# Expert stage: finished rows added straight into the output by an indirect transfer, instead of gathered back at the end

## The reference, cut to what matters

```
top_v, top_i = top_k(softmax(x @ gate_w.T), 2)      # 2 of 8 experts per token
comb_w[token, e] = top_v where e was chosen, else 0
for e in range(8):
    h = silu(x @ w1[e] + b1[e])                     # 512 -> 2048
    y = h @ w2[e] + b2[e]                           # 2048 -> 512
    out = out + y * comb_w[..., e]
t = t + out
```

## Time and profile before

| | |
|---|---|
| median of three runs | 1652.41 us (1646.14 to 1654.00) |
| the profiled execution | 1653.27 us |
| its span, first to last instruction | 1651.7 us |
| expert stage, first block's layer 1 begins | 1151.80 us |
| last matmul of the kernel ends | 1616.01 us (1605.64 + 10.37) |
| PE / DVE / ACT / POOL busy, share of the span | 80% / 67% / 43% / 22% |

### The profile page before, as it was taken

How to read it: one execution, slowest core, us unless ns; L and a number is a source line. 1 busy time by engine, 2 the same in 40 slices (tenths; PEclk the granted TensorE clock), 3 DMA queues, 4 the chain that set the end, 5 groups by cost and what they waited for, 6 DMA issues and landing times.

```text
span 1651.7 us, 34685 instructions
## 1 busy us (share of the span) xinstructions
PE 1327.7 (80%) x12878; PEld 911.1 (55%) x12879; DVE 1107.4 (67%) x1725; ACT 712.4 (43%) x1091; POOL 356.5 (22%) x366
## 2 busy tenths in 40 slices
PE   3734799999358999974659999865999999998991
PEld 1214576765256676642235555452677777776770
DVE  3576888887668888866876666654646775476333
ACT  3236455454545545531263323241646664466330
POOL 0121344544223454340220000005000000000004
PEclk9857899999678999986959999955999999999996
DMA  8042000000310000014021000025436663354005
GB/s 291 30 148 95 2 2 1 1 1 1 130 37 3 1 1 1 1 51 154 25 67 47 1 0 0 0 105 220 170 126 229 224 227 125 129 199 152 25 26 159
DMA packets 34029, 132.31 MB, mean 80 GB/s; under 512 B 6664, under 2 KB 8456, under 8 KB 24016
## 3 DMA queue, kind: packets, MB, share of 16 engines
q1 hardware_dynamic: 25808, 103.19, 17.3%
q0 software_dynamic: 8160, 28.32, 5.0%
HBM read 108.82 MB, written 22.68 MB: 80 GB/s over the span
## 4 chain that ended last, share of the span: by engine, by line
PE 47%; issue 17%; DVE 16%; POOL 11%; DMA 4%; ACT 4%; POOLq 0%; DVEq 0%; SPq 0%; ACTq 0%
PE banks L2138 14%; PE banks L2159 13%; PE banks L1670 5%; PE banks L1700 3%; POOL mb_quad L942 2%; POOL mb_ysq L906 2%; DVE mb_ca L592 2%; POOL mb_quad L934 1%; POOL mb_ring L929 1%; POOL mb_ysq L892 1%; PE banks L1002 1%; POOL xs_table L2171 1%; DVE mb_S L679 1%; PE banks L340 1%; DMA eb_un<-ys_table,eb_slot 1%
## 5 line engine op out<-in xcount | busy, mean ns | idle before, releaser
L2138 PE MATMUL banks<-eb_x_hi,eb_w_hi 128*128 128x128 f16 x1344 | 228.3, 220 | 2.0 <-DVE eb_x_lo L2038 2.0
L2138 PE MATMUL banks<-eb_x_lo,eb_w_hi 128*128 128x128 f16 x1344 | 228.3, 220 | 0.0
L2138 PE MATMUL banks<-eb_x_hi,eb_w_lo 128*128 128x128 f16 x1344 | 228.2, 220 | 0.0
L978 PE MATMUL banks<-mb_u_hi,mb_wi_hi 128*128 (+3 forms) x1152 | 204.2, 223 | 4.8 <-ACT mb_ca L805 4.8
L978 PE MATMUL banks<-mb_u_hi,mb_wi_lo 128*128 (+3 forms) x1152 | 203.8, 222 | 0.0
L978 PE MATMUL banks<-mb_u_lo,mb_wi_hi 128*128 (+3 forms) x1152 | 203.8, 222 | 0.0
L2138 PEld LDWEIGHTS banks<-eb_x_hi,eb_w_hi 128*128 128x128 f16 x1344 | 132.3, 98 | 4.7 <-issue 2.4
L2138 PEld LDWEIGHTS banks<-eb_x_lo,eb_w_hi 128*128 128x128 f16 x1344 | 132.3, 98 | 2.4
L2138 PEld LDWEIGHTS banks<-eb_x_hi,eb_w_lo 128*128 128x128 f16 x1344 | 132.3, 98 | 0.0
L2159 PE MATMUL banks<-eb_w_hi,eb_h_hi 128*128 x336 | 128.4, 382 | 0.0
L2159 PE MATMUL banks<-eb_w_lo,eb_h_hi 128*128 x336 | 128.2, 382 | 0.0
(11 more groups left out here) (437 smaller groups left out, 3238.7 us busy)
## 6 DMA issues: line engine op xcount, KB each, us to landing
eb_raw<-e_w SPq DMA_DIRECT2D x36, 1024.0 KB, 5.0
eb_un<-e_w SPq DMA_DIRECT2D x28, 1024.0 KB, 7.4
mb_ring<-m_in_w SPq DMA_DIRECT2D x8, 1072.0 KB, 5.3
xs_table<-zero POOLq DMA_DIRECT2D x1, 6400.0 KB, 21.1
eb_xg<-xs_table POOLq DMA_DIRECT2D x23, 256.0 KB, 2.9
ys_table<-eb_y POOLq DMA_DIRECT2D x21, 256.0 KB, 6.7
ab_raw<-a_in_w SPq DMA_DIRECT2D x4, 1154.0 KB, 11.7
mb_ring<-m_out_w SPq DMA_DIRECT2D x4, 1024.0 KB, 5.2
```

The lines of the kernel that those rows point to most:

```text
L978: x = e.matmul(ps[0:width, bank, n * P:(n + 1) * P], a[:, k, f:f + width], b[:, k, ds(i * P, P)], start=(k == 0 and m == 0), stop=(k == KD ...
L2138: o = e.matmul(ps[:, j, c * P:(c + 1) * P], a[:, side, k, f * P:(f + 1) * P], b[:, k, :], start=(k == 0 and m == 0), stop=(k == KD - 1 and ...
```

## The change

POOL no longer writes blocks to `ys_table`. It writes each block's 128 rows by an indirect transfer with `compute_op=ALU.add` into the output tensor itself, at the tokens' rows. For that the row's token number and gate must be known in the block's order. They go there by a small table in DRAM, `who_table`, with two numbers (8 bytes) for each slot: DVE puts the gates beside the token numbers in `mine`, POOL scatters them by 16 indirect transfers of 128 x 8 bytes, waits for them, and loads the table back as `who` (128 partitions x 23 blocks x 2). DVE copies a block's token numbers to `row` as integers and multiplies the block by the gates as it leaves PSUM. SP stores the residual tiles to `out` before the blocks instead of at the end; POOL waits for these stores before its first block. Slots that no token fills point, with gate 0, at 128 spare rows behind the output, which the host drops. The first stage fills `who_table` and the spare rows in place of a part of `ys_table`. A fifth small load, `c_mine`, joins the stage's parameter loads, for all of which `par_in` stands.

```diff
@@ zero_tables
-        e.dma_start(self.ys_dram[TOPK * TT * P:(FILLED - 2) * P, :].rearrange("(b p) f -> p b f", p=P),
-                    zero[:].unsqueeze(1).to_broadcast([P, FILLED - 2 - TOPK * TT, D])).then_inc(self.zero_out, 16)
+        e.dma_start(self.who_dram[0:FILLED * P, :], self.ins["c_nobody"]).then_inc(self.zero_out, 16)
+        e.dma_start(self.out[TOK:TOK + P, :], zero[:]).then_inc(self.zero_out, 16)
@@ stage_moe
-    PARS = ((gw, "e_gw"), (b1, "e_b1"), (b2, "e_b2"), (iota, "c_iota"))
+    PARS = ((gw, "e_gw"), (b1, "e_b1"), (b2, "e_b2"), (iota, "c_iota"), (mine, "c_mine"))
@@ sp: between the loads for the second expert and the loop of loads
+        e.wait_ge(b2_done, TT)
+        for i in range(TT):
+            e.dma_start(core.out[i * P:(i + 1) * P, :], t[:, i, :]).then_inc(t_sent, 16)
...
-        for i in range(TT):
-            e.wait_ge(t_done, TOPK * (i + 1))
-            e.dma_start(core.out[i * P:(i + 1) * P, :], t[:, i, :]).then_inc(out_sent, 16)
-        e.wait_ge(out_sent, 16 * TT)
+        e.wait_ge(t_sent, 16 * TT)
@@ dve: behind the plan
+        for k in range(TOPK):
+            x = e.tensor_copy(mine[:, k * TT:(k + 1) * TT, 1], top[:, :, k])
+        x.then_inc(mine_done, 1)
@@ dve: end of a block
+            e.wait_ge(who_in, 16)
             core.apart(e)
-            e.tensor_copy(y[:], ps[:, 5, :]).then_inc(y_ev, 1)
+            e.tensor_copy(row[:], who[:, ds(s, 1), 0])
+            e.tensor_scalar(y[:], ps[:, 5, :], who[:, ds(s, 1), 1], None, ALU.mult).then_inc(y_ev, 1)
@@ dve: behind the blocks
-        for n in range(TOPK * TT):
-            i, k = n // TOPK, n % TOPK
-            e.wait_ge(back[n % TT], 16 * (n // TT + 1))
-            if k:
-                e.wait_ge(t_done, n)
-            e.scalar_tensor_tensor(out=t[:, i, :], in0=un[:, n % TT, :], scalar=top[:, i, k:k + 1], in1=t[:, i, :],
-                                   op0=ALU.mult, op1=ALU.add).then_inc(t_done, 1)
@@ pool: behind fetch(1)
+        e.wait_ge(mine_done, 1)
+        for k in range(TOPK):
+            for i in range(TT):
+                e.indirect_dma_start(out=who_dram, out_offset=bass.IndirectOffsetOnAxis(ap=slot[:, k, i:i + 1], axis=0),
+                                     in_=mine[:, k * TT + i, :], in_offset=None).then_inc(told, 16)
+        e.wait_ge(told, 16 * TT * TOPK)
+        e.dma_start(who[:, 0:MOST, :], who_dram[0:MOST * P, :].rearrange("(b p) c -> p b c", p=P)).then_inc(who_in, 16)
+        e.wait_ge(t_sent, 16 * TT)
@@ pool: block
-            e.dma_start(ys_dram[ds(s * P, P), :], y[:]).then_inc(y_out, 16)
+            e.indirect_dma_start(out=core.out, out_offset=bass.IndirectOffsetOnAxis(ap=row[:, 0:1], axis=0),
+                                 in_=y[:], in_offset=None, compute_op=ALU.add).then_inc(y_out, 16)
@@ pool: behind the blocks
-        for n in range(TOPK * TT):
-            i, k = n // TOPK, n % TOPK
-            if n >= TT:
-                e.wait_ge(t_done, n - TT + 1)
-            e.indirect_dma_start(out=un[:, n % TT, :], out_offset=None, in_=ys_dram[0:(FILLED - 2) * P, :],
-                                 in_offset=bass.IndirectOffsetOnAxis(ap=slot[:, k, i:i + 1], axis=0)).then_inc(back[n % TT], 16)
```

More of the change, by code:

```diff
@@ L59, in __init__ @@
         self.xs_dram = nc.dram_tensor("xs_table", [TABLE * P, D], F32).ap()
-        self.ys_dram = nc.dram_tensor("ys_table", [TABLE * P, D], F32).ap()
+        self.who_dram = nc.dram_tensor("who_table", [TABLE * P, 2], F32).ap()
         self.zero_set, self.zero_out = self.sem("zero_set"), self.sem("zero_out")
@@ L273, in pool @@
         e.wait_ge(added, TT)
-        e.wait_ge(core.zero_out, 32)
+        e.wait_ge(core.zero_out, 48)
     def act(e):
@@ L1818, in stage_moe @@
     y = sb("y", [P, D])
-    xs_dram, ys_dram = core.xs_dram, core.ys_dram
+    mine, who, row = sb("mine", [P, TOPK * TT, 2]), sb("who", [P, TABLE, 2]), sb("row", [P, 1], U32)
+    xs_dram, who_dram = core.xs_dram, core.who_dram
     names = """par_in var_done sd_done un_done turned0 copied0 logits max_done exp_done mask_done ranks table_done plan_done
-         scattered xg_in turned xhi_done xlo_done whi_done wlo_done h_mm h_taken silu_done hhi_done
-        hlo_done y_mm y_ev y_out t_done y_sent out_sent mix_done mix_turned mix_ev b2_mm b2_done dve_own act_own""".split()
+         mine_done told who_in t_sent scattered xg_in turned xhi_done xlo_done whi_done wlo_done h_mm h_taken silu_done hhi_done
+        hlo_done y_mm y_ev y_out y_sent mix_done mix_turned mix_ev b2_mm b2_done dve_own act_own""".split()
     s_ = {n: sem(n) for n in names}
     (par_in, var_done, sd_done, un_done, turned0, copied0, logits, max_done, exp_done, mask_done, ranks, table_done, plan_done,
-     scattered, xg_in, turned, xhi_done, xlo_done, whi_done, wlo_done, h_mm, h_taken, silu_done,
-     hhi_done, hlo_done, y_mm, y_ev, y_out, t_done, y_sent, out_sent, mix_done, mix_turned, mix_ev, b2_mm, b2_done, dve_own, act_own) = \
+     mine_done, told, who_in, t_sent, scattered, xg_in, turned, xhi_done, xlo_done, whi_done, wlo_done, h_mm, h_taken, silu_done,
+     hhi_done, hlo_done, y_mm, y_ev, y_out, y_sent, mix_done, mix_turned, mix_ev, b2_mm, b2_done, dve_own, act_own) = \
         (s_[n] for n in names)
     raw_in = [core.sem(f"e_raw_in{b}") for b in range(EX_RAWS)]
-    back = [sem(f"back{b}") for b in range(TT)]
-    PARS = ((gw, "e_gw"), (b1, "e_b1"), (b2, "e_b2"), (iota, "c_iota"))
+    PARS = ((gw, "e_gw"), (b1, "e_b1"), (b2, "e_b2"), (iota, "c_iota"), (mine, "c_mine"))
     PAR = 16 * len(PARS)
@@ L2301, in shape_constants @@
     c["c_iota"] = np.tile(np.concatenate([np.arange(E), 1 - 2 * (np.arange(E) % 2), np.arange(MOST)]).astype(np.float32), (P, 1))
+    token = np.arange(TT)[None, :] * P + k[:, None]
+    c["c_mine"] = np.tile(np.stack([token, 0 * token], 2), (1, TOPK, 1)).astype(np.float32)
+    c["c_nobody"] = np.tile(np.stack([TOK + k, 0 * k], 1), (FILLED, 1)).astype(np.float32)
     return c
@@ L2347 @@
     ins = {k: nc.dram_tensor(k, v.shape, mybir.dt.from_np(v.dtype), kind="ExternalInput").ap() for k, v in arrays.items()}
-    out = nc.dram_tensor("out", [TOK, D], F32, kind="ExternalOutput").ap()
+    out = nc.dram_tensor("out", [TOK + P, D], F32, kind="ExternalOutput").ap()
     program(nc, ins, out)
     result = run_bass_kernel_spmd(nc, [arrays], core_ids=[0]).results[0]["out"]
-    return np.ascontiguousarray(np.asarray(result).T).reshape(1, SEQ, SIDE, SIDE)
+    return np.ascontiguousarray(np.asarray(result)[:TOK].T).reshape(1, SEQ, SIDE, SIDE)
```

## The result

The changed kernel takes 1639.08 us (median of 12 runs, 1634.01 to 1644.00), beside 1653.91 for the kernel before (12 runs, 1646.14 to 1657.98): a ratio of 0.9914, with an interval of 0.9893 to 0.9934. It is faster by 0.9%, where 1630, or 1.4%, was forecast.

What follows compares the result with a forecast made beforehand. PE sets the pace through the blocks, then 35.7 us of copying, writing, gathering and adding follow. From 1653.27: -27.5 end, +3.0 `who`, +0.3 parameter load, +0.7 gaps, -23.5 in all, giving 1629.8, called 1630; range 1623 to 1645.

Steps and rivals of the forecast that it cites:

- the tail's sum: After the last matmul: steps from 1616.01 add up to 1624.2 instead of 1651.7, gaining 27.5 us, bounds 23.2 to 28.8.
- about 0.3 for the last waits: Kernel's end, behind POOL's loop: the last waits take about 0.3 us, beside 1.94 for leaving the loop.
- stores of the residual ... `t_sent` costs nothing: Before the blocks: SP's 2 MB of stores land long before POOL finishes its scatters, so waiting for them costs nothing.
- longer loop bodies may lengthen the gaps: PE's gaps without a releaser, such as 2.65 and 4.21 us, may grow: 0.7 us added, from 0 to 2.
- Gaps without a releaser that weren't there: In the profile after: listed among the signs that would show the forecast wrong; no size given.
- the table is there in time: Rival, start of the blocks: the table lands by 1184.5, its load needing 8.5 us; total 1626.8, chance 0.25.
- the 3.0 us for `who`: First blocks: `who` lands at 1186.5, PE waits 2.0 us, plus 1 for the clock; bounds 0 to 15.3.
- DVE's train: Start of the blocks: DVE's subtractions from 1170.76 hold the 16th scatter until 1173.9, but not the table load's issue.
- The adding transfer isn't the bound: Each block: the add hides under PE's 21.1 us; the rival, 22 us landings and about 1692, had chance 0.07.
- The table's rival of 1642: Rival, first blocks: the table is slow, PE waits 12.5 us and its clock falls; chance 0.12 with 1636 to 1645.
- the rival of about 1652: Rival: the end hardly shortens, or something else takes the gain; 1645 to 1661, chance 0.06.
- the prediction's own case of 1627 to 1636: Whole kernel: a small wait of PE for the table, forecast 1630 us, chance 0.50.

Runs made afterwards that it cites:

- x1: The changed kernel without the eight stores of the residual, so the output lacks the residual: median 1638.6 us, ratio 0.9916 to the kernel before.
- x5: The changed kernel with each residual store issued as soon as its tile is ready, ahead of the second expert's weight loads: 1630.25 us, ratio 0.9869 to before.
- x8: The changed kernel with early residual stores and a POOL drain in every block together: median 1623.6 us, ratio 0.9832 to the kernel before.
- x4: The changed kernel with the residual stores issued later, once PE has turned block 1: 1630.01 us, ratio 0.9878 to the kernel before.
- x2: The changed kernel without the 16 short scatters of token and gate, all rows then going to spare rows: 1629.47 us, one execution.
- x11: The changed kernel, unchanged, profiled once more: 1640.16 us, one execution.
- x7: The changed kernel with the blocks' rows scattered without the add, so the sum is left out: 1629.97 us, one execution.
- x6: The changed kernel with a POOL drain in every block, between the fetch and the wait for y: median 1628.03 us, ratio 0.9872 to before.
- x9: The changed kernel with early stores, drains in every block and no table, token and gates riding in `xs_table` rows: median 1625.35 us, ratio 0.9820 to before.
- x10: The kernel before, unchanged, profiled once more: 1646.38 us, one execution.

## Why the prediction was right or wrong

The end, the mechanism. The 16 gathers went as worked out, and the first half of the tail's sum holds: from the last matmul to the empty bank 1.25 (predicted 1.19), leaving the loop 1.9 (1.94). POOL's issue came 1.07 after the copy (0.76). The adding transfer took 4.7, beside the 4.0 chosen between 2.7 and 8.3. The Trainium skill, Collectives: The Full Stack, on SDMA and CCE, led to an estimate of 4.05. The landings of the last transfer, 4.7 with the add and 2.8 without, are a ratio of 1.7 where it would be 1.5; 0.6 of the 1.9 between them is issue, so that less than this speaks of the datapath.

**The step that failed at the end** is "about 0.3 for the last waits": behind the loop stands POOL's drain, and it cost 5.7, with 0.3 beside it. In the kernel before that drain was already there and ended beside the last store, so the chain didn't show it; its row is longer, 14.1 us from 1637.3, but POOL was still issuing gathers until 1643.6, so that less than this is clearing up. With it the gain at the end is 20.7, not 27.5, and it falls outside the bounds of 23.2 to 28.8, which moved only the transfer. The difference of 6.8 is 5.7 of drain, 0.7 of transfer, 0.3 of handing over and 0.1 of rounding.

**The step that failed at the start** is "stores of the residual ... `t_sent` costs nothing", and with it the 16 scatters, which were counted by POOL's time alone. Nobody waited for the stores' semaphore, that part was right. But the question was asked only of who waits for them, not of what else travels by the DMA engines. The term "longer loop bodies may lengthen the gaps", 0.7 with a bound of 2, named the right gap with the wrong cause: it is 4.3 to 4.8 longer, and what follows it is slower too, up to 7.0 in all. That second part the prediction knew and put elsewhere: it has layer 2 slower by 2.16 behind a gap of 4.21, at a granted clock of 0.53, but it charged this only to the wait for `who` and took the gap of 2.65 for one that costs nothing behind it. "Gaps without a releaser that weren't there" was given as a sign that the forecast is wrong, and it is what appeared.

**The table.** POOL's scatters went as predicted, 0.96 + 0.30 each, but for the 1 us that DVE's short subtractions were to add: the longest is 1.04. The load was issued at 1176.81 (predicted 1176.0). The rival "the table is there in time" is the one that came true: the load took 5.0, with 1.5 of issue, not 10.5, so the 3.0 us for `who` were none. The 32 ns for each 8-byte run were too much: the trace has the 2944 runs in 48 packets of 448 or 512 bytes, of 0.14 to 0.56 us each. The rest is luck: SP issued the next weights only at 1180.01, 3.2 behind the start of the load, since PE's longer gap had held DVE up. Where they come 0.4 to 0.9 behind it, the load takes 7.4, 7.8 and 8.1 (x1, x5, x8), and 9.7 in x4 (0.4 ahead of it, behind the late stores), near the 10.5. The last scatter wasn't held up by DVE's train, since that came later (1177.53) than before: a term that was right only while everything else stood still. The 4.23 us that POOL waited for the scatters to land (1.7 predicted) and a stage that began 1.5 later stand in its place, so that the start agrees by errors that cancel. The load's issue wasn't held by DVE's train: 1.54 us, with the train from 1177.53 on beside most of it, for 1.50 in x2, where it ran without one.

**The rest.** The parameter load, 0.3, is 0: what PE does there isn't later. The adding transfer isn't the bound, with 21.1 us of cover for at most 8.3; row copy and scale hide under PE. The table's rival of 1642 and the rival of about 1652 did not occur in their way, though the second one's form ("something else takes the gain") describes what happened at half its size.

Two of the prediction's bounds are a little off in themselves: 28.8 moves only the transfer, and without most of the row copy it would be 29.0; and with 20 us for each microsecond the 27.5 of the end last to a landing of 20.3, the 20.1 being for the net gain.

The sum after the event, against -23.5: end -20.7, start of the blocks +7.0 (of which 2.2 are the clock), stage begun later +1.5, parameter load and table 0: -12.2. The missing half is two terms, 6.8 and 7.0, of which neither is a wait on a semaphore. The 4.0 us that the prediction added for the table, the parameter load and the gaps didn't occur, and hid that much of the two. That 1639.08 lies within 1623 to 1645 is in part luck: it is outside the prediction's own case of 1627 to 1636, in the stretch that was held by a slow table, and the table wasn't slow.

Still open: by what the stores hold the instruction transfers up and the short scatters stretch them; why the clock stayed up behind the gap in one profile of 13; what lowers it in the attention-like block in some executions and not in others; and what in POOL's earlier transfers the drain works off (with plain scatters it took 6.35).

## What to carry to other kernels

When work moves from the end into a quiet stretch, ask what comes through that stretch besides what waits for a semaphore: an engine that jumps over a long piece of its program for the first time may stop until code has come by DMA. Without the 16 short scatters and the 2 MB of stores the gap was 2.5, with the one 3.8 to 4.4, with the other 4.7 to 5.9, with both up to 7.5, though nobody waits for either, and the clock then takes up to 2.6 more (x8). When two kernels are compared by profile, look at the granted clock of the stretch before, too: it moved the start of this stage by up to 10 us. When the last transfers of an engine become the end of the program, look for the instructions behind the loop that the chain of waits never showed, such as a drain, and do their work inside the loop, where it is covered. Two numbers for each row cost PE less when they were carried in the row itself than in a table of their own (a gap of 2.49 for 3.80), though the times of the two kernels can't be told apart.

## What the runs showed of the hardware

- POOL's drain depends on what POOL's transfers have left behind: 5.70 us at the end of this kernel and of x1, x4, x5 and x11 (6.35 in x7), 5.05 in x2 with 16 transfers fewer, 0.14 where each block drained (x6, x8, x9). In the loop the longest is 8.13 in x6, 10.11 in x8 and 3.72 in x9, which has no short scatters; the median is 3.0 to 3.1, with one fetch on its way.
- PE's first jump over the `Else` part of its block takes 3.4 to 3.5 us with the DMA engines quiet and 8.4 with stores and short scatters on them. PE starts 1.8 us after the last "instruction" transfer has ended, in 12 of 13 profiles. That transfer of 0.02 MB lasts 0.9 to 1.1 us alone or among stores, and 2.2 to 2.9 among 8-byte scatters.
- Behind a gap of 2.5 us or more in its matmuls PE ran at a granted clock of about 0.5 for some microseconds (0.52 for 3.3 us in x9 and x10, for 4.6 in the changed kernel); behind the gap of 2.65 in the first profile of before it did not.
- With PE busy for 139 of 140 us the granted clock was 0.94 or 0.95 in five profiles and 1.00 in eight, for the same work.
- An indirect transfer of 128 rows from POOL takes 0.96 us of issue at 8 bytes a row as at 2 KB a row; with an add 1.59, and 1.00 for the same rows without it (x7). Landing with nothing beside it: 2.8 plain, 4.7 with the add, in 80 and 144 packets.
- 2944 runs of 8 bytes from DRAM, in 48 packets, were loaded in 5.0 us, 1.54 of it issue, and in 7.4 to 9.7 with 1 MB weight loads beside them.
